# Graph layer and mixture of experts on one core: norm arithmetic on DVE, rows summed in memory, scatters on 128 partitions, three dense gelu buffers

## The chip, the cores and the metric

The kernel runs on one core of a Trainium2 chip. The metric is the device time of one execution in microseconds (us), the median of several runs. The engines are PE (TensorE), DVE (VectorE), ACT (ScalarE), POOL (GpSimd) and SP (SyncE, which here only issues transfers).

## What is computed

From the reference, cut to what matters. The adjacency matrix is dense in storage, 10000 x 10000 in float32, some 400 MB, and it is read once.

```python
x = x + relu(adj @ (item_feat @ W_item.T + b_item) + (layernorm(x) @ W_user.T + b_user))   # x: 10000 x 128
z = layernorm(x)
probs = softmax(z @ gate_w + gate_b)              # 8 experts
cw = the two largest probs of each row, elsewhere 0
for e in range(8):
    y = gelu(z @ W1[e] + b1[e]) @ W2[e] + b2[e]   # 128 -> 256 -> 128
    x = x + cw[:, e:e+1] * y
```

## The kernel before

**Blocks and chunks.** The 10000 rows are cut into 20 blocks of 500 (UB). For a block, the product with the adjacency runs over 26 chunks (CH), each of three slabs of 128 items; there are 520 chunks in all (NCH), numbered n, with b = n // 26 the block and c = n % 26 the position in it. For each chunk SP loads 750 KB into one of six buffers (`load_raw`, L296), ACT rounds it to a high part (`hi_chunk`, L738, the activation at L742, three buffers), DVE subtracts to get the low part (`lo_chunk`, L948, L952, two buffers), and PE does nine matmuls into one PSUM bank (`agg_chunk`, L487: three slabs times high x high at L496 and high x low at L497, then three times low x high at L501). ACT may start a chunk when PE is done with the chunk three before, DVE when PE is done with the one two before. SP may load chunk n once DVE is done with chunk n - 6.

**Everything else is threaded between the chunks.** All engines run the same loop over n, and constants give the position c of each other step: L54 to L57, and from L66 on the lists for the expert tiles. Steps of the block just finished (`post`, L681 on PE, L885 on ACT, L1198 on DVE) go beside the chunks of the next one. In their order: x1 is made on DVE at 1, turned and multiplied with the gate on PE at 1, its statistics taken on DVE at 4 (`stats2`, L980, L987) and those of the next block's input at 5 (`stats1`, L966, L971). POOL works out variance, power and shift of both in one call (`rstd`, L1289): eleven operations on 125 x 8 numbers, L1304 to L1320, of which L1316 is the power of -1/2. At 11 DVE takes the gate's logits (`logits`, L995, first operation L998), POOL raises e to them (`power`, L1322, L1324), ACT normalizes the rows at 12 (`ln2_norm`, L776, L787) and the next block's input at 15 (`ln1_norm`, L754), DVE does the softmax at 16 (L1011), the first and the second expert at 17 and 18 (`top`, L1029), and the slot numbers at 21 (`slots`, L1065). The rows of the blocks 0 to 16 (S = 17) are then scattered by expert into memory by POOL, eight indirect DMAs of 125 rows a block (`scatter`, L1339, L1346).

**Expert tiles.** Blocks 0 to 11 are one group, blocks 12 to 16 another. When a group's rows are scattered, a table of tiles is made on DVE (`table`, L1086), SP fills the gaps behind each expert's rows (`fill_end`, L374; it waits for all scatters of the group; at `FILL_AT`, L66), and tiles of 512 rows of one expert are worked off: 31 beside blocks 13 to 18, 17 beside blocks 18 and 19, the chunk of each in `W1_AT`. A tile is loaded by SP (`load_zt`, L342, weights and bias by `load_w`, L327, four bias buffers), turned on PE (`tile_turn`, L575), and goes through the first layer (`first_layer`, L583), gelu on ACT, second layer, and a turn back; DVE scales it (`y_out`, L1156, L1161, which waits for the sends of the tile two before), and POOL sends its rows to the array `rr` in memory by four indirect DMAs of 128 rows (`send`, L1351, L1355).

**The end.** Blocks 17 to 19 are done densely: 24 steps (ND), one for each block and expert (`dense_gelu`, L848; `scale`, L1168, L1172; `dense_round`, L860; `dense_rest`, L1174, L1176; on PE `first_layer` with L589 to L591, `dense_wbc`, L634, with L643, and `dense_w2`, L646, with L662 to L664). The gelu's output `dg` has two buffers. Beside them the two results of each row of the blocks 0 to 16 are summed: SP loads 256 KB of x1 (`comb_load`, L356), POOL adds two ranks of `rr` by an adding DMA each (`comb_add`, L1326, L1336), and SP stores the sum (`comb_store`, L365), 17 times; the dense blocks are stored by `out_store` (L370).

**What sets the order.** Every engine works through its own list in the order written, and waits are on semaphores, so a wait holds everything behind it on that engine.

Of the kernel before, what the change touches and what calls it, by code (L numbers as in the profile page):

```python
# [101 lines left out]
def build(nc, adj, adj_tail, x_tok, x_t, feat_t, feat_tail, wi_t, bb, bsel_d, wu_t, gate_w, gate_b,  # L102
          w12, b12, b2, ident_d, tri_d, w8_d, base_d, dest_d, sel_d, ints_d, out_s, out_d, zs, rr):
    ctx = ExitStack()
    with ctx:
# [27 lines left out]
        bias = sb("bias", [P, 4, 3])  # L133
# [35 lines left out]
        consts = sb("consts", [P, 4, 2 * SUBS])  # L169
# [5 lines left out]
        tsl = sb("tsl", [P, 2, SUBS, E])  # L175
        idx = sb("idx", [P, 2 * SUBS], I32)
# [36 lines left out]
        bn1_made, bn2_made, rs_step, rs_made = sem("bn1_made"), sem("bn2_made"), sem("rs_step"), sem("rs_made")  # L213
        ln1_normed, ln1_turned, ln1_copied, ln2_normed = (
# [31 lines left out]
        def dg(d):  # L246
            return g[:, 0:2 * UB] if d % 2 else flat[:, 0:2 * UB]
# [47 lines left out]
        def _(sp):  # L295
# [59 lines left out]

            def comb_load(p):  # L356
                if p == 0:
                    sp.wait_ge(lo_made, NCH)
# [5 lines left out]

            def comb_store(p):  # L365
                sp.wait_ge(comb_added[p % CB], 32 * (p // CB + 1))
                sp.dma_start(out_s[p * T:(p + 1) * T, :].rearrange("(p s) d -> p (s d)", s=SUBS), comb(p))\
                    .then_inc(comb_stored[p % CB], 16)
# [77 lines left out]
            for j in range(ND + 5):  # L446
                for p in range(S):
                    if COMB_OUT[p] == j:
                        comb_store(p)
# [495 lines left out]
        def _(dve):  # L945
# [275 lines left out]
            for n in range(LAST):  # L1221
# [47 lines left out]
                if d == 1:  # L1269
                    stats2(BLOCKS - 1)  # L1270
# [212 lines left out]
```

## Time and profile before

| | |
|---|---|
| median of 3 runs | 1539.0 us (1538.3 to 1539.04) |
| the profiled execution | 1538.6 us, of which the span of its instructions 1536.8 us |
| PE busy | 1469.6 us, 96% of the span |
| DVE, ACT, POOL busy | 1248.4, 1095.3, 885.7 us |
| transfers | 498.06 MB, 324 GB/s over the span |

The profile tells one execution. Times in it are microseconds from the first instruction. A line such as L952 is a line of the kernel; the releaser in brackets is what ended the idle time before an instruction. A matmul's record includes its way through the array, so matmuls overlap in the records, and the pace is the distance of their starts. Several buffers of one name are shown under one name.

### The profile page before, as it was taken

What the parts mean: (1) busy time and instruction counts of PE and PEld (TensorE: products, weight loads), DVE (VectorE), ACT (ScalarE), POOL (GpSimd) and SP (SyncE); (2) the same over time, 40 slices, a digit from 0 to 9 for tenths busy, and PEclk for the clock granted to TensorE, in tenths of its full rate; (3) what the DMA queues carried; (4) which work ended last, traced back from release to release, by engine and by line L of the source; (5) the groups of instructions that cost most, each with busy time, mean ns of one, the idle gap of its engine ahead of it and who ended that gap; (6) DMA issues with size and microseconds to landing.
All of it is one profiled execution on the core that took longest, in us unless ns stands there. A gap on an engine that the chain in (4) does not pass through costs nothing.

```text
span 1536.8 us, 20551 instructions
## 1 busy us (share of the span) xinstructions
PE 1469.6 (96%) x6682; PEld 1172.5 (76%) x6682; DVE 1248.4 (81%) x1627; ACT 1095.3 (71%) x1162; POOL 885.7 (58%) x630
## 2 busy tenths in 40 slices
PE   8999999999999999999998798999999999999997
PEld 6777787877877877778776587888888887877664
DVE  4778788888887887888888687889898988888775
ACT  4567677677677676776774677788887878788664
POOL 0105735637557457456364148777887887587662
PEclk9999999999999999999999899999999999999999
DMA  8879999999999999999997987889898899888399
GB/s 327 303 302 348 366 360 361 377 345 344 378 347 354 364 345 364 363 344 384 338 350 262 371 315 271 332 327 337 327 335 326 327 338 331 287 274 283 110 219 229
DMA packets 141720, 498.06 MB, mean 324 GB/s; under 512 B 33024, under 2 KB 39120, under 8 KB 141614
## 3 DMA queue, kind: packets, MB, share of 16 engines
q1 hardware_dynamic: 119694, 466.12, 82.3%
q0 software_dynamic: 21920, 30.64, 7.6%
q8 instruction: 53, 0.87, 0.2%
q14 instruction: 53, 0.43, 0.1%
HBM read 460.22 MB, written 36.31 MB: 323 GB/s over the span
## 4 chain that ended last, share of the span: by engine, by line
PE 49%; DVE 15%; POOL 14%; issue 8%; ACT 7%; DMA 5%; SPq 2%; POOLq 0%; ACTq 0%; DVEq 0%
PE p_agg L501 13%; PE p_agg L496 11%; PE p_agg L497 11%; DVE s_a_lo L952 9%; ACT s_a_hi L742 4%; POOL s_rs L1316 3%; DMA s_raw<-rr 3%; POOL s_rs L1304 2%; POOL zs L1346 2%; POOL s_rs L1312 1%; POOL s_rs L1305 1%; PE p_hid L478 1%; PE p_hid L589 1%; PE p_hid L591 1%; PE p_hid L590 1%
## 5 line engine op out<-in xcount | busy, mean ns | idle before, releaser
L952 DVE TENSOR_TENSOR s_a_lo<-s_raw,s_a_hi 128x1500 fp32r<-128x1500 f32 x520 | 885.8, 1718 | 139.4 <-PE p_agg L501 84.4
L742 ACT ACTIVATE s_a_hi<-s_raw 128x1500 fp32r<-128x1500 f32 x520 | 750.1, 1454 | 207.9 <-PE p_agg L501 184.9
L496 PE MATMUL p_agg<-s_a_hi,s_h_hi 128*128 128x500 f32 x1560 | 630.6, 404 | 10.2 <-ACT s_a_hi L742 10.1
L497 PE MATMUL p_agg<-s_a_hi,s_h_lo 128*128 128x500 f32 x1560 | 611.7, 392 | 0.0
L501 PE MATMUL p_agg<-s_a_lo,s_h_hi 128*128 128x500 f32 x1560 | 449.3, 396 | 33.9 <-DVE s_a_lo L952 31.0
L1346 POOL DMA_INDIRECT zs<-s_rows,s_idx x136 | 231.9, 1705 | 306.3 <-DVE s_idx L1080 211.8
L501 PEld LDWEIGHTS p_agg<-s_a_lo,s_h_hi 128*128 128x128 f32 x1560 | 290.2, 190 | 120.2 <-DVE s_a_lo L952 63.3
L496 PEld LDWEIGHTS p_agg<-s_a_hi,s_h_hi 128*128 128x128 f32 x1560 | 297.4, 191 | 75.3 <-ACT s_a_hi L742 17.9
L497 PEld LDWEIGHTS p_agg<-s_a_hi,s_h_lo 128*128 128x128 f32 x1560 | 297.3, 191 | 57.9 <-issue 3.2
L1355 POOL DMA_INDIRECT rr<-s_ysb,s_dests x192 | 277.4, 1445 | 102.7 <-issue 53.1
L1324 POOL TENSOR_TENSOR s_gt<-s_ebase,s_gt 125x32 f32<-125x32 f32 x20 | 130.8, 6538 | 37.2 <-DVE s_gt L1006 37.1
L1304 POOL TENSOR_TENSOR s_rs<-s_bn 125x8 f32<-125x8 f32 (+1 forms) x21 | 42.2, 2010 | 113.6 <-DVE s_bn L971 104.3
L1154 DVE TENSOR_TENSOR s_gl<-s_g,s_gh 128x1024 fp32r<-128x1024 f32 x48 | 58.8, 1226 | 51.3 <-ACT s_gh L832 51.3
L825 ACT ACTIVATE s_g<-p_hid,s_bias 128x512 f32<-128x512 f32 x96 | 60.6, 684 | 48.5 <-PE p_hid L591 48.5
L832 ACT ACTIVATE s_gh<-s_g 128x1024 fp32r<-128x1024 f32 x48 | 50.9, 1060 | 9.3 <-PE p_y L607 8.1
L1316 POOL TENSOR_TENSOR s_rs<-s_rs,s_consts 125x8 f32<-125x8 f32 (+1 forms) x21 | 55.7, 2655 | 1.6
L838 ACT ACTIVATE s_yt<-p_y,s_bias 128x512 f32<-128x512 f32 x48 | 32.6, 680 | 31.4 <-PE p_y L607 31.4
L787 ACT ACTIVATE s_rows<-p_agg,s_rs 125x128 f32<-125x128 f32 x80 | 30.0, 456 | 34.1 <-POOL s_rs L1320 34.1
L1336 POOL DMA_DIRECT2D s_raw<-rr x34 | 31.0, 1134 | 32.8 <-DMA s_raw<-out_s 16.7
L746 ACT ACTIVATE s_h_hi<-p_hid 128x384 fp32r<-128x384 f32 x26 | 12.8, 491 | 41.2 <-PE p_hid L478 41.2
L589 PE MATMUL p_hid<-s_zh,s_wt 128*128 128x512 f32 (+1 forms) x102 | 41.7, 409 | 0.4 <-ACT s_g L857 0.4
L818 ACT ACTIVATE s_zh<-p_tp 128x512 fp32r<-128x512 f32 x48 | 28.2, 587 | 19.0 <-PE p_hid L591 17.2
(214 smaller groups left out, 1478.6 us busy)
## 6 DMA issues: line engine op xcount, KB each, us to landing
s_raw<-adj SPq DMA_DIRECT2D x520, 750.0 KB, 6.6
s_wraw<-w SPq DMA_DIRECT2D x56, 256.0 KB
s_zt<-zs SPq DMA_DIRECT2D x48, 264.0 KB, 3.1
s_raw<-rr POOLq DMA_DIRECT2D x34, 256.0 KB, 6.7
s_xtok<-x_tok SPq DMA_DIRECT2D x20, 256.0 KB, 5.6
s_xt<-x_t SPq DMA_DIRECT2D x20, 250.0 KB, 6.7
zs<-s_early SPq DMA_DIRECT2D x18, 264.0 KB, 5.7
out_s<-s_x1s SPq DMA_DIRECT2D x17, 256.0 KB, 6.5
```

What stands on the lines that cost most here:

```text
L496: mm(o, h_hi[:, k * D:(k + 1) * D], hi, start=(k == 0), stop=False)
L497: mm(o, h_lo[:, k * D:(k + 1) * D], hi, start=False, stop=False)
L501: last = mm(o, h_hi[:, k * D:(k + 1) * D], a_lo[:, n % LOS, j * UB:(j + 1) * UB], start=False, stop=False)
L742: fn(a_hi[:, n % HIS, :], raw[:, n % RAW, :], ACT.Copy).then_inc(hi_made, 1)
L825: fn(g[:, h * T:(h + 1) * T], hid[h][:, :], ACT.Gelu, bias=bias[:, k % 4, h:h + 1])\
L952: tt(a_lo[:, n % LOS, :], raw[:, n % RAW, :], a_hi[:, n % HIS, :].bitcast(F32), ALU.subtract)\
L1154: tt(gl[:, :], g[:, :], gh[:, :].bitcast(F32), ALU.subtract).then_inc(gl_made, 1)
L1304: tt(row[0], even, odd, ALU.add)
L1316: tt(row[1], row[5], mhalf, ALU.pow).then_inc(rs_step, 1)
L1324: gp.tensor_tensor(gt[0:TS, 2, :], ebase[0:TS, :], gt[0:TS, 1, :], ALU.pow).then_inc(ez_made, 1)
L1346: gp.indirect_dma_start(out=zs[:, :], out_offset=bass.IndirectOffsetOnAxis(ap=idx[0:TS, j:j + 1].bitcast(U32), axis=0), in_=rows[k][0:TS, ...
L1355: gp.indirect_dma_start(out=rr[:, :], out_offset=bass.IndirectOffsetOnAxis(ap=dests[:, k % XR, s:s + 1].bitcast(U32), axis=0), in_=yrows(k ...
```

## The change

It does four things. The arithmetic of the norms, except the power, moves from POOL to DVE (`variances` and `shifts`, seven operations where POOL did ten), and the steps of a block behind it move forward: statistics of the input at 3, variances at 4, shifts at 7, logits at 8, rows normalized at 9, input normalized at 11, softmax 12, experts 13 and 14, slots 17. The sums of the rows are no longer made through SBUF at the end: POOL adds `rr` onto the output in memory, group 0 in six pieces of two blocks for each rank beside the tiles of group 1, the rest at the end in one piece for each rank. Scatters take 128 partitions, the last three rows going to spare rows past the end. The dense gelu gets a third buffer. With these go six bias buffers instead of four, and new places for fills, tiles and their loads; the first tile is at chunk 347 instead of 352, the first of group 1 at 477 instead of 482.

```diff
-X1_AT, X1T_AT, BN2_AT, BN1_AT, X1S_AT, LG_AT, LN2_AT = 1, 1, 4, 5, 4, 11, 12
-TAILHI_AT, TAILLO_AT, SOFT_AT, TOP1_AT, TOP2_AT, LN1_AT = 9, 10, 16, 17, 18, 15
-PREFIX_AT, LN1T_AT, SLOT_AT, LN1C_AT = 19, 17, 21, 20
-TABLE_AT = (21, 22, 23)
+X1_AT, X1T_AT, X1S_AT, BN1_AT, BN2_AT, FIN_AT, LG_AT, LN2_AT = 1, 1, 4, 3, 4, 7, 8, 9
+TAILHI_AT, TAILLO_AT, SOFT_AT, TOP1_AT, TOP2_AT, LN1_AT = 6, 7, 12, 13, 14, 11
+PREFIX_AT, LN1T_AT, SLOT_AT, LN1C_AT = 15, 13, 17, 16
+TABLE_AT = (17, 18, 19)
...
-FILL_AT = [(hi + 1) * CH + 6 for lo, hi in GROUPS]
-FIRST_W1 = [at + E // 2 + 4 for at in FILL_AT]
+FILL_AT = [(hi + 1) * CH + 4 for lo, hi in GROUPS]
+FIRST_W1 = [at + E // 2 + 1 for at in FILL_AT]
...
-W_LOAD = [0, 0] + [w + (6 if o + 2 < NTG[0] else 4) for o, w in enumerate(W1_AT[:NT - 2])] + [NCH - 3, NCH - 2]
-ZT_LOAD = [0, 0] + [max(W1_AT[k - 2] + 3, FILL_AT[k >= NTG[0]] + E // 2) for k in range(2, NT)]
-COMB_AT = [p if p < GROUPS[1][0] else p + 3 for p in range(S)]
-COMB_OUT = [6 + p if p < GROUPS[1][0] else p + 10 for p in range(S)]
+W_LOAD = [0, 0] + [w + 5 for w in W1_AT[:NT - 2]] + [NCH - 3, NCH - 2]
+ZT_LOAD = [0, 0] + [max(W1_AT[k - 2] + 5, FILL_AT[k >= NTG[0]] + E // 2) for k in range(2, NT)]
...
-            return g[:, 0:2 * UB] if d % 2 else flat[:, 0:2 * UB]
+            return (flat[:, 0:2 * UB], g[:, 0:2 * UB], flat[:, 2 * UB:4 * UB])[d % 3]
...
-                if d >= 2:
-                    act.wait_ge(gl_made, o - 1)
+                if d >= 3:
+                    act.wait_ge(gl_made, o - 2)
...
+            def variances(j):
...
+                tt(row[3], even, odd, ALU.subtract)
+                tt(row[4], bn[0:TS, lo:hi, 2], bn[0:TS, lo:hi, 5], ALU.add)
+                tt(row[0], even, odd, ALU.add).then_inc(rs_step, 1)
+                dve.wait_ge(rs_step, 2 * j + 1)
+                nc.vector.tensor_scalar(row[4], row[4], 1.0 / D, EPS, ALU.mult, ALU.add)
+                nc.vector.scalar_tensor_tensor(out=row[3], in0=row[3], scalar=0.25, in1=row[3],
+                                               op0=ALU.mult, op1=ALU.mult).then_inc(rs_step, 1)
+                dve.wait_ge(rs_step, 2 * j + 2)
+                tt(row[5], row[3], row[4], ALU.add).then_inc(var_made, 1)
+
+            def shifts(j):
...
+                dve.wait_ge(pow_made, j + 1)
...
+                nc.vector.scalar_tensor_tensor(out=rs[0:TS, 2, lo:hi], in0=rs[0:TS, 1, lo:hi], scalar=-0.5,
+                                               in1=rs[0:TS, 0, lo:hi], op0=ALU.mult, op1=ALU.mult)\
+                    .then_inc(rs_made, 1)
...
+            def add_rank(i, k):
+
+                blocks = GROUPS[0][1] // PAIRS
+                first, last = (i * blocks, (i + 1) * blocks) if i < PAIRS else GROUPS[1]
+                if k == 0:
+                    pool.wait_ge(rr_zeroed, 16 * 3)
+                    pool.wait_ge(x1_stored, 16 * last)
+                    for j in range(2):
+                        pool.wait_ge(sent[j], 16 * SUBS * tiles_of(j, NTG[0] if i < PAIRS else NT))
+                else:
+                    pool.wait_ge(rank0_added, 16 * (PAIRS + (i == PAIRS)))
...
+                gp.dma_start(out, new, max_dma_last_dim=8192, accum_op=ALU.add).then_inc((rank0_added, rank1_added)[k], 16)
...
-                            out_offset=bass.IndirectOffsetOnAxis(ap=idx[0:TS, j:j + 1].bitcast(U32), axis=0),
-                            in_=rows[k][0:TS, s, :], in_offset=None).then_inc(scattered, 16)
+                            out_offset=bass.IndirectOffsetOnAxis(ap=idx[:, j:j + 1].bitcast(U32), axis=0),
+                            in_=rows[k][:, s, :], in_offset=None).then_inc(scattered, 16)
...
                     if YOUT_AT[k] == n:
                         send(k)
-                        if k == NT - 3:
-                            rstd(BLOCKS)
...
+                        i = k - NTG[0] - 1
+                        if 0 <= i < 2 * PAIRS:
+                            add_rank(i % PAIRS, i // PAIRS)
+            power_of_rs(BLOCKS)
+            power(BLOCKS - 1)
+            add_rank(PAIRS, 0)
+            add_rank(PAIRS, 1)
```

## Rows read from the trace of the kernel before

**Rows 1.** Stretch: us, PE, PEld, DVE, ACT, POOL busy (instructions), clock, DMA share, GB/s.
```profile
98.70:762.10 663.40, 641.54 (x2872) 518.83 (x2871) 557.95 (x671) 468.51 (x418) 360.69 (x215) 0.99 0.96 358
...
824.50:910.40 85.90, 74.84 (x324) 59.03 (x323) 60.80 (x83) 55.98 (x59) 28.24 (x23) 0.94 0.84 309
...
1328.70:1434.00 105.30, 102.97 (x504) 82.72 (x502) 87.77 (x126) 84.19 (x108) 80.92 (x63) 1.00 0.76 256
```

**Rows 2.** Timeline of DVE in block 4: start us, us, line, tiles, idle before.
```profile
279.43 1.72 DVE L952 TENSOR_TENSOR s_a_lo<-s_raw,s_a_hi 128x1500 fp32r<-128x1500 f32 x1 [0.32 <-PE p_agg L501]
...
291.58 0.89 DVE L987 BATCH_NORM_STATS2 s_bn<-p_agg 125x6 f32<-125x128 f32 x4
...
308.55 0.19 DVE L998 TENSOR_TENSOR s_gt<-p_small,s_rs 125x32 f32<-125x32 f32 x1 [2.20 <-POOL s_rs L1320]
...
321.99 0.19 DVE L1034 TENSOR_TENSOR s_gt<-s_gt,s_w 125x32 f32<-125x32 f32 x1
...
339.50 1.72 DVE L952 TENSOR_TENSOR s_a_lo<-s_raw,s_a_hi 128x1500 fp32r<-128x1500 f32 x1 [0.30 <-PE p_agg L501]
```

**Rows 3.** Timeline of PE in block 4.
```profile
297.13 0.83 PE L501 MATMUL p_agg<-s_a_lo,s_h_hi 128*128 128x500 f32 x3
...
299.15 0.85 PE L501 MATMUL p_agg<-s_a_lo,s_h_hi 128*128 128x500 f32 x3
...
311.10 0.95 PE L501 MATMUL p_agg<-s_a_lo,s_h_hi 128*128 128x500 f32 x3 [1.59 <-DVE s_a_lo L952]
```

**Rows 4.** Timeline of POOL in block 4.
```profile
294.95 3.23 POOL L1304 TENSOR_TENSOR s_rs<-s_bn 125x8 f32<-125x8 f32 x1 [2.23 <-DVE s_bn L971]
...
304.74 3.14 POOL L1316 TENSOR_TENSOR s_rs<-s_rs,s_consts 125x8 f32<-125x8 f32 x1
...
309.49 6.84 POOL L1324 TENSOR_TENSOR s_gt<-s_ebase,s_gt 125x32 f32<-125x32 f32 x1 [1.04 <-DVE s_gt L1006]
```

**Rows 5.** Timeline of SP and of ACT in block 13.
```profile
838.73 1.49 SPq L379 DMA_DIRECT2D zs<-s_early  x2
...
858.05 9.20 SPq L299 DMA_DIRECT2D s_raw<-adj  x7
...
846.85 1.45 ACT L742 ACTIVATE s_a_hi<-s_raw 128x1500 fp32r<-128x1500 f32 x1 [8.74 <-DMA s_raw<-adj]
```

**Rows 6.** Timeline of DVE in block 14.
```profile
927.93 0.69 DVE L1161 TENSOR_TENSOR s_ysb<-p_y,s_probs 128x512 f32<-128x512 f32 x1 [5.80 <-DMA rr<-s_ysb,s_dests]
```

**Rows 7.** Timeline of the dense end, ACT and PE.
```profile
1517.57 1.25 ACT L857 ACTIVATE s_raw<-p_hid,s_dbias 128x500 f32<-128x500 f32 x2 [1.51 <-DVE s_h_hi L1176]
...
1521.25 1.25 ACT L857 ACTIVATE s_g<-p_hid,s_dbias 128x500 f32<-128x500 f32 x2 [1.50 <-DVE s_h_hi L1176]
...
1516.42 0.49 PE L643 MATMUL p_y<-s_cw,s_selr 16*128 16x500 f32 x1
...
1518.39 0.47 PE L589 MATMUL p_hid<-s_a_hi,s_h_lo 128*128 128x500 f32 x1
```

**Rows 8.** Timeline of the last us, DVE and SP.
```profile
1527.91 0.68 DVE L1181 TENSOR_TENSOR s_xt<-p_y,s_xt 128x500 f32<-128x500 f32 x1 [1.88 <-PE p_y L664]
...
1533.97 0.43 SPq L372 DMA_DIRECT2D out_d<-s_xt  x1
```

**Rows 9.** POOL: timeline of a block's scatters, and the page's group of sends.
```profile
814.36 1.29 POOL L1346 DMA_INDIRECT zs<-s_rows,s_idx  x1 [15.28 <-DVE s_idx L1080]
...
823.99 3.32 POOL L1346 DMA_INDIRECT zs<-s_rows,s_idx  x1 [5.71 <-issue]
...
834.37 1.19 POOL L1346 DMA_INDIRECT zs<-s_rows,s_idx  x1 [0.31 <-issue]
...
L1355 POOL DMA_INDIRECT rr<-s_ysb,s_dests x192 | 277.4, 1445 | 102.7 <-issue 53.1
```

**Rows 10.** The software queue on the page (packets, MB, share), and six us of block 4.
```profile
q0 software_dynamic: 21920, 30.64, 7.6%
...
297.40:303.40 6.00, 6.00 (x28) 5.02 (x27) 5.37 (x4) 4.68 (x5) 5.84 (x7) 1.00 1.02 412
```

More of the change, by code:

```diff
@@ L132, in build @@
         wt = sb("wt", [P, 3, 2, 2 * HID], F32R)
[L133 removed]
+        bias = sb("bias", [P, BIAS, 3])
         dbias = sb("dbias", [P, E, 3])
@@ L445, in _ @@
             load_w(NT + 3)
[L446 to L449, printed above, removed]
-                for p in range(S):
-                    if COMB_AT[p] == j:
-                        comb_load(p)
+            for j in range(ND + 4):
                 if j + 4 < E:
@@ L457, in _ @@
             sp.wait_ge(stored, 16 * (BLOCKS - S))
-            for i in range(CB):
-                sp.wait_ge(comb_stored[i], 16 * ((S - 1 - i) // CB + 1))
+            sp.wait_ge(rank0_added, 16 * (PAIRS + 1))
+            sp.wait_ge(rank1_added, 16 * (PAIRS + 1))
         @block.tensor
@@ L824, in gelu @@
                 for h in range(2):
-                    fn(g[:, h * T:(h + 1) * T], hid[h][:, :], ACT.Gelu, bias=bias[:, k % 4, h:h + 1])\
+                    fn(g[:, h * T:(h + 1) * T], hid[h][:, :], ACT.Gelu, bias=bias[:, k % BIAS, h:h + 1])\
                         .then_inc((gelu_half, gelu_done)[h], 1)
@@ L837, in y_evac @@
                     act.wait_ge(y_turned, k)
-                fn(yt[:, :], y[0][:, :], ACT.Identity, bias=bias[:, k % 4, 2:3]).then_inc(yt_made, 1)
+                fn(yt[:, :], y[0][:, :], ACT.Identity, bias=bias[:, k % BIAS, 2:3]).then_inc(yt_made, 1)
             def dz_round(q):
@@ L1243, in _ @@
                             .then_inc(b2_split, 1)
+                if n < NCH and c == BN1_AT + (4 if b == 0 else 0):
+                    stats1(b)
                 if b >= 1 and n < NCH:
@@ L1324, in power @@
                 gp.tensor_tensor(gt[0:TS, 2, :], ebase[0:TS, :], gt[0:TS, 1, :], ALU.pow).then_inc(ez_made, 1)
[L1326 to L1327 removed]
+            def add_rank(i, k):
+                blocks = GROUPS[0][1] // PAIRS
+                first, last = (i * blocks, (i + 1) * blocks) if i < PAIRS else GROUPS[1]
+                if k == 0:
                     pool.wait_ge(rr_zeroed, 16 * 3)
[L1329 to L1337 removed]
+                    pool.wait_ge(x1_stored, 16 * last)
[3 more added lines that the diff above has]
+                    pool.wait_ge(rank0_added, 16 * (PAIRS + (i == PAIRS)))
+                rows_of = slice(first * T, last * T), slice(k * RANK + first * T, k * RANK + last * T)
+                out, new = (t[rows, :].rearrange("(p s) d -> p (s d)", p=P) for t, rows in zip((out_s, rr), rows_of))
+                gp.dma_start(out, new, max_dma_last_dim=8192, accum_op=ALU.add).then_inc((rank0_added, rank1_added)[k], 16)
             def scatter(p):
@@ L1394, in _ @@
                         send(k)
-                        if k == NT - 3:
-                            rstd(BLOCKS)
-            for first, last in ((0, GROUPS[1][0]), (GROUPS[1][0], S)):
-                for p in range(first, last + 2):
-                    if p < last:
-                        comb_add(p, 0)
-                    if p - 2 >= first:
-                        comb_add(p - 2, 1)
-                    if p == 4:
-                        power(BLOCKS - 1)
+                        i = k - NTG[0] - 1
[5 more added lines that the diff above has]
+            add_rank(PAIRS, 1)
 def kernel(**inputs):
```

123 lines of the change are left out of this document (50 added, 73 removed).

## The prediction

> **What bounds the kernel now.** I read the busy time by stretch first. In blocks 1 to 11 PE is busy 641.5 of 663.4 us at a granted clock of 0.99, in block 19 103.0 of 105.3 us, but in block 13 only 74.8 of 85.9 us at 0.94 [rows 1]. So PE's own work sets the time, and a change can gain only what PE still waits for. Four such places matter here.
>
> *Blocks 1 to 12.* DVE's low-part subtractions mark the chunks. Block 4 runs from 279.43 to 339.50 us: 60.1 us for 26 chunks [rows 2]. A chunk that waits for nothing takes PE 2.02 us (the L501 groups at 297.13 and 299.15), 26 of them 52.9 us [rows 3]; the transposes, gate products, prefix sums and tail of a block come to about 3.1 us in the same timeline. So some 4.1 us of each block are waits and restarts. The largest is one of 1.59 us at 311.10, on DVE [rows 3]. DVE had itself idled 2.20 us before the gate's first operation, until POOL's L1320 [rows 2]. POOL's normalization takes eleven tiny operations, from 294.95 until just before the gate's 308.55: 13.5 us, of which L1304 takes 3.23 and the power of L1316 3.14 [rows 4]. About 3.5 of the 4.1 us come through DVE (this wait, and three bursts of gate operations later).
>
> *Blocks 13 and 14.* SP stops for the scatters before it fills the gaps in memory, and only at 838.73 issues the first fill; ACT waits 8.74 us for a chunk at 846.85; the seven chunk loads held behind SP's fills, weights and tile loads go from 858.05 on [rows 5]. In block 14 DVE waits 5.80 us to overwrite a row buffer that POOL, busy with a scatter, sends late [rows 6].
>
> *The dense end.* Its step is 3.68 us: ACT's gelu waits 1.51 us for DVE to finish with one of the two gelu buffers [rows 7].
>
> *The last us.* DVE's last result is ready at 1528.6, but its store is issued at 1533.97, behind the stores of the summed rows; the span ends at 1536.8 [rows 8].
>
> **Part by part.** *Norm arithmetic.* POOL keeps one power of some 3.1 us; DVE gets seven operations. One such operation takes 0.19 us [rows 2], some 0.22 with the gap behind it; three of the seven need nothing and overlap: about 0.9 us a block. They stand at chunks 4 and 7, the gate now starts at chunk 8, its softmax follows at 12, the tops at 13 and 14. POOL's power of the exponentials takes 6.84 us [rows 4], inside the four chunks (8.1 us) left for it; before, five. Does DVE keep up? Back to back it needs 1.64 us a chunk where PE needs 2.03, so it gains 0.4 a chunk, and since it works two buffers ahead it may be 1.7 us late before PE notices (one chunk and six matmuls, 3.4, less its own 1.7). Lateness after each chunk: 3 (statistics, 0.8, [rows 2]) 0.4; 4 (statistics and the new arithmetic, 1.6) 1.6; 6, 0.8; 7 (tail 0.7, shift 0.1) 1.2; 8 (gate 0.8) 1.6; 11, 0.4, raised to 1.1 by ACT, which now normalizes at 9 and 11 (2.1 and 1.6 us); 12 (softmax 0.9) 1.6; 13 (top, 1.2) 2.1 with PE's transposes taken off; 14 (1.0) 2.3. Over the limit of 1.7 that is 1.0 us of waiting, 1.4 with restarts. So 3.5 becomes 1.4: 2.1 us x 12 blocks = **25 us**. Ends: 0.5 a block if the denser bursts give most of it back (6), all of 3.5 (42).
>
> *Scatters on 128 rows, eight positions 17 instead of 21.* Before, the eight of a block take 21 us, from 814.36 to 835.6, with one pause of 5.71 us for no engine [rows 9]; the sends, with 128 rows, take 1.45 us each and idle 53.1 us in 192 for no engine, 0.3 each [rows 9]. Bounds for a block's eight: 14 us like the sends, 21 as now; I take 14, since the sends are the same operation in shape. The three added rows an operation go to spare rows and are 2.4% more packets. [...]
>
> *Start of the tiles.* The scatter now starts four chunks (8 us) earlier and ends 6 earlier still, while SP asks two chunks (4 us) sooner: its 11 us wait goes away, or shrinks to about 6. What stays is SP's own issue time: some 19 us from the first fill to the load at 858.05, for five chunks that PE would do in 10 [rows 5]. Of about 16 us lost here I take back **8** (3 with scatters as now, 12 at best). The send behind the scatter is now ahead of it (positions 354 and 355): the 5.80 us wait goes, with PE's slow restart **5** (0 to 6).
>
> *Rows summed in memory.* Removed: 34 adding DMAs, 17 loads and 17 stores of 256 KB. Added: beside group 1's tiles twelve adding DMAs of 512 KB in memory, and two of 1.3 MB at the end. POOL pays about 1 us to issue one; it has 9.4 us for a tile against 7.0 for four sends, so that is covered, as is the wait of the second rank for the first. The DMA engines are the open cost. Plain transfers reach 412 GB/s at a full share: 2.4 us a MB. The software queue moved 30.64 MB in 7.6% of the span, 117 us, 3.8 a MB; were all above 2.4 due to the 8.9 MB of additions, these would cost 7.2 [rows 10]. I take 5.5, midway between those two: 35 us for 6.3 MB in about 105 us of blocks 18 and 19. These need 256 GB/s, 0.62 of the DMA time at the best rate (0.76 as recorded, [rows 1]). 0.62 and 0.33 make 0.95: nearly full, with six chunk buffers as a cushion. I charge **4 us** (0 to 24: 0.76 and 0.47 make 1.23).
>
> *Three gelu buffers.* The loop gelu, scale, rest of 3.6 us opens to two steps. Next is PE: 1.97 us from L643 at 1516.42 to L589 at 1518.39 [rows 7] and six matmuls at the 0.225 of a chunk's nine, 1.35: 3.32; I take 3.35. DVE has 2.23 and ACT 2.1 us a step, about 3 with the weights. The first four steps stay DVE's (row outputs, statistics, weights, now 0.9 more). 19 steps x 0.33 = 6.3, less 2.2 of transposes and bias products that the old waits covered, and 1.3 at the last item: **5.5** (2 to 14 if the step falls to 3.0). The last norm's power now waits on POOL for the last sends, to about 1450; DVE needs it at about 1453: covered by 3 us.
>
> *The end.* The last store follows DVE by 0.1 us instead of 5.4: **5** (3 to 6). The two late additions (2.6 MB, 14 to 19 us from about 1467) end 25 us ahead.
>
> *At nothing:* the index DMA and copy in block 0, six bias buffers instead of four (they take waits from SP), tiles moved five chunks forward (the same PE work); the tile load is placed two chunks later, which leaves it 10 us for 3, and if that cover goes PE stands for the difference per tile.
>
> **Sum.** 25 + 8 + 5 - 4 + 5.5 + 5 = 44.5 us off the profiled run's 1538.6 (span 1536.8), 0.4 below the median 1539.0: 1494; some 1 us more where DVE's small waits in blocks 15 to 18 go. **1493 us**, 3.0% faster.
>
> **Rivals.**
> *A, the norm's wait only moves.* Three bursts, now nearer to each other, and DVE at about 93% of PE's pace, speak for it; the walk above against. 0.5 a block: 1493 + 19 = 1512.
> *B, full queues in blocks 1 to 12.* The DMA share there is 0.96 at 358 GB/s [rows 1], and 58 us a block needs 371; were the queues full, the block could not shorten: 1493 + 25 = 1518. But six us at 412 GB/s stand in the same blocks [rows 10]. [...]
> *C, the DMA queues fill in blocks 18 and 19.* At 7.2 to 8 us a MB 10 to 25 us lost: 1503 to 1518.
> *D, slower than before.* [...] At x us a MB the loss is 6.3x less the idle 40 us; 1539 is passed from x = 14, twice the upper bound. At 16 it is 61 us: 1550.
> *E, more is gained.* Scatters, fills and dense steps all at their good ends, DVE never late: 1475.
> *F, the change doesn't do what it says:* POOL, still held by DMA issue, delivers the power after chunk 7, DVE's shift waits as the gate did, and the start of the tiles stays: 1520.
>
> **Chances.** Forecast 0.55 (its own range 1482 to 1504), A 0.11, B 0.04, C 0.09, D 0.04, E 0.10, F 0.04, no change at all 0.03. A measurement of this kernel can tell about 0.2%, 3 us. Faster 0.93, within 0.2% 0.03, slower 0.04. The range takes in the forecast, A, B and C, and E down to 1475: **1475 to 1518**.
>
> **What would show it.** Blocks 1 to 12 at about 58.0 us, with no DVE wait on POOL before the gate; DVE bursts at chunks 13 and 14 as PE's only waits; scatters without the 6 us pause; ACT's waits for chunk loads in block 13 below 6 us in all; dense steps of 3.35 us; the last store within 0.5 us of DVE's last result; block 19 with a DMA share near 0.95 and no ACT wait for chunks. A block still at 60, or chunk waits of ACT in blocks 18 and 19, would make it wrong.

## The result and the profile after

The changed kernel takes 1501.1 us (median of four runs, 1501.0 to 1506.6) against 1538.7 for the kernel before on the same chip (1536.0 to 1539.0): a ratio of 0.977, 95% interval 0.974 to 0.979. Forecast were 1493 us and a range of 1475 to 1518. The profiled run took 1501.0 us with a span of 1499.2; the sum of the prediction had said 1494.

I cut both traces where DVE subtracts the first low part of a block. "Tiles" is the stretch from there in block 13 to the start of the last subtraction of all; "end" is the rest of the span.

| us, profiled runs | before | after | gained | forecast |
|---|---|---|---|---|
| block 0 | 87.5 | 84.3 | 3.2 | 0 |
| blocks 1 to 12 | 725.8 | 696.6 | 29.2 | 25 |
| tiles, blocks 13 to 19 | 604.7 | 610.8 | -6.1 | 8 + 5 - 4 + 1 |
| end | 107.5 | 96.1 | 11.4 | 5.5 + 5 |

The time came out within 0.6% of the forecast partly by luck: the tiles missed by 16.1 us and had the wrong sign, and 8.3 us of that were made up by block 0 (3.2), by blocks 1 to 12 (4.2) and by the end (0.9). The busy time by stretch for the changed kernel: blocks 1 to 11, then 13, 14, 18 and 19 (stretch: us, PE, PEld, DVE, ACT, POOL busy, clock, DMA share, GB/s).

```profile
95.70:732.90 637.20, 632.36 (x2873) 514.04 (x2872) 566.42 (x749) 466.91 (x419) 262.82 (x109) 1.00 0.98 370
792.30:877.60 85.30, 76.25 (x345) 61.10 (x344) 64.81 (x95) 59.39 (x65) 29.48 (x19) 0.96 0.92 334
877.60:956.30 78.70, 78.64 (x381) 65.05 (x380) 69.60 (x105) 64.14 (x75) 56.26 (x34) 1.00 0.95 329
1202.90:1303.40 100.50, 91.81 (x432) 74.08 (x430) 78.98 (x119) 73.01 (x90) 61.00 (x40) 0.98 0.89 311
1303.40:1403.10 99.70, 92.48 (x446) 73.83 (x445) 79.97 (x123) 75.79 (x97) 72.04 (x54) 1.00 0.92 290
```

Eleven blocks take 637.2 us where they took 663.4 [rows 1], each 57.9. But block 13 is as long as before; with the tiles five chunks earlier it also holds 345 matmuls where it held 324 [rows 1]. In blocks 18 and 19 PE stands idle for 8.7 and 7.2 us, with the granted clock at 0.98 and 1.00. Over all the tiles PE has the same 2765 matmuls before and after (busy 584.2 and 582.0 us), and its idle time rises from 20.6 to 28.8 us.

The norm's steps in block 4, on POOL and on DVE, are to be read beside [rows 2, 4]:

```profile
283.49 3.08 POOL L1313 TENSOR_TENSOR s_rs<-s_rs,s_mhalf 125x8 f32<-125x8 f32 x1 [13.52 <-DVE s_rs L982]
291.69 6.84 POOL L1318 TENSOR_TENSOR s_gt<-s_ebase,s_gt 125x32 f32<-125x32 f32 x1 [5.12 <-DVE s_gt L1011]
```

```profile
282.59 0.17 DVE L974 TENSOR_TENSOR s_rs<-s_bn 125x8 f32<-125x8 f32 x1
...
283.24 0.17 DVE L982 TENSOR_TENSOR s_rs<-s_rs 125x8 f32<-125x8 f32 x1
...
290.76 0.18 DVE L1003 TENSOR_TENSOR s_gt<-p_small,s_rs 125x32 f32<-125x32 f32 x1
```

POOL's 13.5 us have become 3.1, DVE's six operations last 0.8 us, and the gate's first operation follows with no wait on POOL. PE's waits for DVE in blocks 1 to 11 (us in total, times, longest), before and after:

```profile
PE p_agg L501 <- DVE s_a_lo L952: 20.4, 19, 1.9
```

```profile
PE p_agg L476 <- DVE s_a_lo L927: 3.6, 11, 0.3
```

The wait of 1.6 us that every block had at its chunk 12 is gone; what is left is 0.3 us at chunk 15.

PE's waits at the start of the two groups of tiles are new. The column in brackets is PE's idle time and what ended it; below it is the load that the last of them waits for.

```profile
820.04 1.12 PE L555 MATMUL p_tp<-s_ident,s_zt 128*128 128x128 f32 x4 [4.99 <-DMA s_zt<-zs]
...
1227.45 0.66 PE L555 MATMUL p_tp<-s_ident,s_zt 128*128 128x128 f32 x4 [1.45 <-DMA s_zt<-zs]
...
1244.18 0.66 PE L555 MATMUL p_tp<-s_ident,s_zt 128*128 128x128 f32 x4 [4.26 <-DMA s_zt<-zs]
```

```profile
1234.85 0.34 SPq L346 DMA_DIRECT2D s_zt<-zs  x1
```

The rows of that tile arrive 9.3 us after their load is issued. And the end, ACT's gelus, DVE's last result and SP's last store [rows 7, 8]:

```profile
1479.17 1.25 ACT L832 ACTIVATE s_raw<-p_hid,s_dbias 128x500 f32<-128x500 f32 x2 [1.45 <-PE p_hid L566]
1482.48 1.24 ACT L832 ACTIVATE s_raw<-p_hid,s_dbias 128x500 f32<-128x500 f32 x2 [1.14 <-PE p_hid L566]
```

```profile
1495.83 0.68 DVE L1186 TENSOR_TENSOR s_xt<-p_y,s_xt 128x500 f32<-128x500 f32 x1 [1.87 <-PE p_y L639]
```

```profile
1496.54 0.33 SPq L352 DMA_DIRECT2D out_d<-s_xt  x1
```

The step is 3.31 us instead of 3.68, ACT now waits for PE and no longer for DVE, and the span ends 2.7 us behind DVE's last result instead of 8.2.

### The profile page after: what moved, and what is told of

It reads as the page before. It is cut to its first block, busy times and chain, and to the rows that moved or that the text cites. A ratio compares the mean times of both kernels' runs of the same rounds, so it can differ in the third digit from the quotient of the medians.

```text
span 1499.2 us, 20455 instructions
## 1 busy us (share of the span) xinstructions
PE 1451.7 (97%) x6682; PEld 1165.8 (78%) x6682; DVE 1263.0 (84%) x1775; ACT 1093.4 (73%) x1162; POOL 709.5 (47%) x397
## 4 chain that ended last, share of the span: by engine, by line
PE 67%; DVE 12%; ACT 8%; issue 7%; DMA 3%; SPq 2%; POOL 1%; ACTq 0%; DVEq 0%; POOLq 0%
PE p_agg L476 17%; PE p_agg L471 15%; PE p_agg L472 15%; DVE s_a_lo L927 8%; ACT s_a_hi L717 4%; PE p_hid L564 2%; PE p_hid L566 2%; PE p_hid L565 2%; ACT s_xtok L733 2%; ACT s_rows L762 1%; PE p_hid L453 1%; PE p_y L580 1%; PE p_y L582 1%; PE p_y L581 1%; PE p_agg L487 1%
## 5 line engine op out<-in xcount | busy, mean ns | idle before, releaser
L476 PEld LDWEIGHTS p_agg<-s_a_lo,s_h_hi 128*128 128x128 f32 x1560 | 287.1, 188 | 97.4 <-DVE s_a_lo L927 40.2
L1351 POOL DMA_INDIRECT rr<-s_ysb,s_dests x192 | 274.1, 1427 | 165.1 <-DVE s_ysb L1166 111.6
L1313 POOL TENSOR_TENSOR s_rs<-s_rs,s_mhalf 125x8 f32<-125x8 f32 (+1 forms) x21 | 56.2, 2678 | 232.6 <-DVE s_rs L982 232.5
L800 ACT ACTIVATE s_g<-p_hid,s_bias 128x512 f32<-128x512 f32 x96 | 60.7, 686 | 44.2 <-PE p_hid L566 38.7
L813 ACT ACTIVATE s_yt<-p_y,s_bias 128x512 f32<-128x512 f32 x48 | 32.9, 685 | 31.4 <-PE p_y L582 23.4
L555 PE MATMUL p_tp<-s_ident,s_zt 128*128 128x128 f32 x192 | 29.6, 278 | 15.8 <-DMA s_zt<-zs 10.7
L564 PE MATMUL p_hid<-s_zh,s_wt 128*128 128x512 f32 (+1 forms) x102 | 41.6, 408 | 0.4 <-issue 0.4
L566 PE MATMUL p_hid<-s_zl,s_wt 128*128 128x512 f32 (+1 forms) x102 | 40.2, 394 | 0.0
L565 PE MATMUL p_hid<-s_zh,s_wt 128*128 128x512 f32 (+1 forms) x102 | 40.1, 393 | 0.0
```

The source lines that it names most:

```text
L476: last = mm(o, h_hi[:, k * D:(k + 1) * D], a_lo[:, n % LOS, j * UB:(j + 1) * UB], start=False, stop=False)
L564: mm(hid[h][:, 0:n], w_hi, hi, start=True, stop=False)
L565: mm(hid[h][:, 0:n], w_lo, hi, start=False, stop=False)
L566: last = mm(hid[h][:, 0:n], w_hi, lo, start=False, stop=True)
L800: fn(g[:, h * T:(h + 1) * T], hid[h][:, :], ACT.Gelu, bias=bias[:, k % BIAS, h:h + 1])\
L1351: gp.indirect_dma_start(out=rr[:, :], out_offset=bass.IndirectOffsetOnAxis(ap=dests[:, k % XR, s:s + 1].bitcast(U32), axis=0), in_=yrows(k ...
```

## The experiments

Twelve kernels ran, each with three rounds beside the kernel before. Ratios are to the kernel before on the same chip (1535.8 to 1537.9 us there); stretches are those of the table, from the profiled run. Kernels 1 and 2 are built on the kernel before, the others on the changed one.

**1. The norm part alone.** The kernel before, with `variances`, `shifts` and the power as in the change and the four lines of positions from X1_AT to TABLE_AT (VAR_AT is BN2_AT); nothing else.

```diff
-                    if c == BN1_AT:
-                        rstd(b)
+                    if c == VAR_AT:
+                        power_of_rs(b)
```

> The kernel before with the norm arithmetic on DVE and the steps of a block at their new positions; fills, tiles, loads, scatters on 125 rows, sums through SBUF and two gelu buffers as before. Theory (the norm part gives the whole gain of blocks 0 to 12): blocks 1 to 12 take 696 to 700 us as in the changed kernel (before 725.8), block 0 84.3 (before 87.5); the scatters come 8 us earlier too, so SP's first fill in block 13 and the send in block 14 no longer wait, some 8 to 13 us. In all 1538.6 - 29 - 3 - 10 = 1497, 1490 to 1505. Rival (part of the gain of blocks 1 to 12 comes from the other parts, fewer scatter packets and the pause): blocks 1 to 12 stay above 705 us, in all 1507 to 1515.

1498.0 us, ratio 0.974 (0.970 to 0.977). Block 0 86.0, blocks 1 to 12 696.6, tiles 597.3, end 106.4, span 1498.1. So the norm part by itself is as fast as the whole change: 38.7 us of span, 29.2 in blocks 1 to 12 and 7.4 among the tiles.

```profile
97.90:735.00 637.10, 632.22 (x2873) 513.96 (x2872) 566.53 (x749) 466.97 (x419) 261.44 (x109) 1.00 0.99 370
794.40:876.30 81.90, 72.89 (x326) 57.43 (x325) 61.63 (x90) 56.31 (x59) 28.10 (x16) 0.98 0.91 334
1291.70:1391.70 100.00, 97.16 (x479) 79.22 (x478) 85.50 (x130) 83.15 (x106) 74.61 (x49) 1.00 0.78 262
```

The theory held (1497 expected). Its blocks 1 to 11 equal the changed kernel's within 0.1 us, so neither the scatters' width nor their packets play a part there. The other three parts of the change then give 10.3 us in the end and lose 13.5 among the tiles. Most of the remaining experiments look for these 13.5.

**2. The arithmetic without the moves.** As 1, every step at its old place.

```diff
+VAR_AT, FIN_AT = 5, 9
```

> The kernel before with the norm arithmetic on DVE alone; every step stays at its old position (variances at 5, shifts at 9, gate at 11). Theory (the wait of DVE for POOL before the gate is what the block lost; the moved steps only start the scatters earlier): blocks 1 to 12 as short as with the moved steps, 58.0 to 58.4 us each, the start of the tiles as before, 1538.6 - 28 = 1510. Rival (the steps' new spacing carries part of it): blocks at 58.8 to 59.5 us, in all 1518 to 1526.

1502.3 us, 0.979 (0.974 to 0.983). That is faster than both expectations (1510, and 1518 to 1526). Blocks 1 to 12 take 693.3 us, less than with the moved steps, and the first eleven of them 57.6 each.

```profile
96.00:729.70 633.70, 629.45 (x2872) 516.23 (x2871) 563.88 (x748) 467.76 (x418) 250.05 (x105) 1.00 1.00 374
```

The gain of the blocks is the arithmetic's; the moves cost 3.3 us there. What they bring is at the tiles, 606.0 against 597.3: the scatters end earlier, and SP waits for them 7.8 us in kernel 1 and 12.9 here. The DMA share of 1.00 at 374 GB/s, in a shorter block than the change has, also disposes of rival B.

**3. No additions beside the tiles.** The rows of blocks 0 to 11 stay unsummed in the output.

```diff
-                        if 0 <= i < 2 * PAIRS:
+                        if False:
```

> The changed kernel without the twelve additions of group 0 beside group 1's tiles; the rows of blocks 0 to 11 in out_s are left unsummed, the two additions at the end stay. Theory (the additions cost what was charged, about 4 us, by load on the DMA engines): the stretch of blocks 18 and 19 up to the last subtraction, 200.2 us, falls to 196, in all 1497. Rival 1 (they are the reason of the stage's extra 14 us of PE waits): the stretch falls to 186 to 190, in all 1488 to 1491. Rival 2 (they cost nothing; the waits come from the tiles' places): the stretch stays within 1.5 us of 200.2, in all 1500 to 1501.

1504.2 us, 0.979 (0.975 to 0.982). Blocks 18 and 19 take 102.7 and 99.6 us (with the additions 100.5 and 99.7):

```profile
1203.20:1305.90 102.70, 92.77 (x432) 74.91 (x431) 79.12 (x120) 73.08 (x90) 60.26 (x38) 0.97 0.85 298
1305.90:1405.50 99.60, 92.39 (x446) 73.77 (x445) 79.83 (x122) 75.70 (x97) 64.09 (x44) 1.00 0.70 234
```

Leaving the additions out gains nothing; the two blocks even take 202.3 us instead of 200.2, and the whole 3 us more. That is outside every range expected (rival 2 had 1.5 us around 200.2), and rival 2, that the additions cost nothing, is the one that it fits; where the 2 us come from is not shown. The additions do load the DMA engines: the shares 0.89 and 0.92 fall to 0.85 and 0.70, by the trace 24.9 us of full load for 6.3 MB, 4.0 us a MB. There was room for that. ACT's waits for chunks in block 18 are 4.0 us without the additions and 2.7 with them, and in block 19 there are none in either.

**4. The first tiles three chunks later.**

```diff
-FIRST_W1 = [at + E // 2 + 1 for at in FILL_AT]
+FIRST_W1 = [at + E // 2 + 4 for at in FILL_AT]
```

> The changed kernel with the first tile of each group three chunks later behind the fills (8 chunks as before the change, now 5), the tile loads still 5 chunks behind the tile two before. Theory (PE turned the first tiles before SP had loaded them): the PE waits for the rows of a tile at 814.7 (4.99 us) and at 1225.6 and 1239.5 (1.45 and 4.26 us) go, in all -8 us, 1493. The tiles of group 1 then stand 2.24 instead of 2.41 chunks apart, which may give back 2: 1493 to 1496. Rival (the waits come from the tile load placed two chunks later, not from the first tile): one of the three goes at most, 1499 to 1503.

1496.4 us, 0.973 (0.970 to 0.976). As the theory said, the three waits at the groups' starts are gone. The tiles fall from 610.8 to 604.9 us; block 18 from 100.5 to 92.5, while block 19 rises to 102.3 and has 2.4 us of waits for rows (3.4 in both blocks, not the 3.9 of the next expectation). The edit also makes the distances of group 1's tiles more even (three of 3 chunks instead of six), so it does not price the first tiles' place alone. The end was 100.8 us in the profiled run, which was the slowest of four (1494.9 to 1500.5).

**5. As 4, and the tile loads two chunks earlier.**

```diff
-ZT_LOAD = [0, 0] + [max(W1_AT[k - 2] + 5, ...
+ZT_LOAD = [0, 0] + [max(W1_AT[k - 2] + 3, ...
```

> The changed kernel with the first tiles 3 chunks later and the tile loads 3 instead of 5 chunks behind the tile two before; only the fills stay 2 chunks earlier than before the change (and with them the first tile, 350 instead of 352). From block 13 to the last subtraction the changed kernel takes 610.7 us, with the first tiles 3 later 604.9, with all places as before 592.4. Theory (the late tile loads are most of what is left, in blocks 18 and 19, where PE still waits 3.9 us for rows): 597 to 601. Rival 1 (the early fills are it: SP asks for the scatters two chunks early and holds the chunk loads behind them, so block 13 stays at 81.8 instead of 77.4): 600 to 604.9. Rival 2 (both together only): 592 to 596.

1495.6 us, 0.973 (0.971 to 0.975). PE waits for no rows any more, yet the tiles take 604.2 us: the waits for rows gave way to waits for DVE (next experiment). The number lies in the range of rival 1, but its cause, the early fills, is only a part at most: block 13 takes 80.1 us where the old places give 77.4, and the next experiment finds more elsewhere.

**6. As 5, and group 1's tiles at an even distance.**

```diff
-... (NCH - 2 - FIRST_W1[1]) / NTG[1]]
+... 36 / NTG[1]]
```

> The kernel with the first tiles 3 later and the tile loads 3 behind (stretch from block 13 to the last subtraction 604.2 us, of it blocks 18 and 19 92.5 and 103.4), with group 1's tiles 36/17 = 2.12 chunks apart instead of 2.24: one distance of 3 chunks among them instead of three (the changed kernel has six, all places as before one). Theory (PE's waits for DVE's low part of the rows and for DVE's scaled tile, 3.5 and 3.2 us in block 19, come where the distances change between 2 and 3 chunks): block 19 falls to 100 to 101 us though it holds no fewer tiles, the two waits to 3 us together, in all 1492. Rival (what is left of the 12 us to the old places comes from the fills two chunks earlier and group 0's tiles alone): block 19 stays at 103 or more, in all 1495 to 1496.

1492.5 us, 0.973 (0.970 to 0.976), the profiled run 1489.0. Against 5 the intervals overlap, so the time alone shows no gain and the reading rests on the trace. Block 19 falls from 103.4 to 98.5 us, below the 100 to 101 expected. PE's waits there (us in total, times, longest), first for 5, then for 6:

```profile
PE p_tp L555 <- DVE s_zl L1144: 3.5, 2, 2.6
PE p_y L590 <- DVE s_ysb L1166: 3.2, 1, 3.2
```

```profile
PE p_y L590 <- DVE s_ysb L1166: 1.2, 2, 0.8
PE p_tp L555 <- DVE s_zl L1144: 0.8, 1, 0.8
```

I read it so: where the distance between tiles is 3 chunks once and 2 the next time, steps of two tiles meet in one chunk and PE waits for DVE. The changed kernel has six such distances of 3 among group 1's sixteen, the kernel before had one.

**7. All places of fills, tiles and loads as before the change.** Norm, additions, scatters and gelu buffers stay changed.

```diff
-FILL_AT = [(hi + 1) * CH + 4 for lo, hi in GROUPS]
+FILL_AT = [(hi + 1) * CH + 6 for lo, hi in GROUPS]
```

and with it the old lines for `FIRST_W1`, `W_LOAD` and `ZT_LOAD`.

> The changed kernel with the places of fills, first tiles, weight loads and tile loads as before the change (fills 2 chunks later, first tile 8 instead of 5 chunks behind them, tile loads 3 chunks behind the tile two before); norm, additions in memory, scatters, three gelu buffers and six bias buffers as changed. The norm alone, with the old places, had 597.3 us from block 13 to the last subtraction, the changed kernel 610.7. Theory (the places alone cost those 13 us): the stretch takes 596 to 600 us, the dense end stays at 96, in all 1501 - 13 = 1488, 1485 to 1491. Rival (the wider scatters, the additions or the sixth bias buffer have a share): the stretch stays at 604 or more, in all 1494 to 1501.

1490.9 us, 0.970 (0.969 to 0.972). The tiles take 592.4 us, 18.4 less than in the changed kernel and below the 596 to 600 expected; the whole gains only 10 us, in part because the end takes 100.3 us instead of 96.1 (see 12).

```profile
793.50:870.90 77.40, 71.42 (x322) 56.78 (x322) 61.52 (x89) 56.38 (x60) 25.61 (x15) 0.98 0.94 350
1194.10:1285.90 91.80, 89.80 (x429) 72.74 (x427) 79.51 (x121) 72.62 (x89) 51.66 (x34) 1.00 0.92 332
1285.90:1386.00 100.10, 97.24 (x479) 79.28 (x478) 85.45 (x131) 83.28 (x106) 80.40 (x60) 1.00 0.98 315
```

SP's first fill is issued at 798.70, with fills placed two chunks later than in the changed kernel, where it is at 798.87. So the scatters decide when filling begins, and asking earlier only means that SP waits 7.5 us for them instead of 2.1, with the chunk loads behind it (11.1 before the change).

**8. Two gelu buffers.**

```diff
-            return (flat[:, 0:2 * UB], g[:, 0:2 * UB], flat[:, 2 * UB:4 * UB])[d % 3]
+            return g[:, 0:2 * UB] if d % 2 else flat[:, 0:2 * UB]
```

> The changed kernel with two gelu buffers in the dense end, as before. Theory (the third buffer gave about 6 us, the earlier last store 5): the 48 gelus, 79.6 us from first to last in the changed kernel, take 85 to 87, and the kernel 1507. Rival 1 (PE's clock falls in the end for want of work, and the third buffer gave more through that): 88 us or more, in all 1510 or more. Rival 2 (the step of the dense end was set by the sums' transfers, now gone): the gelus take 81 us or less, in all 1502.

1514.4 us, 0.985 (0.983 to 0.986). The gelus take 86.7 us from first to last instead of 79.6, the end 103.0 instead of 96.1. The step is 3.68 again:

```profile
1491.78 1.25 ACT L832 ACTIVATE s_raw<-p_hid,s_dbias 128x500 f32<-128x500 f32 x2 [1.51 <-DVE s_h_hi L1181]
...
1495.46 1.25 ACT L832 ACTIVATE s_g<-p_hid,s_dbias 128x500 f32<-128x500 f32 x2 [1.51 <-DVE s_h_hi L1181]
```

The gelus take what the theory said (85 to 87), but the whole is 7 us above its 1507. The third buffer is worth 6.9 us in the end; the rest of this run's distance, 6.6 us, lies elsewhere: block 0 took 87.7 us and the tiles 613.8, by the same instructions as in the changed kernel.

**9. The rows summed through SBUF at the end.** `comb_load`, `comb_add` and `comb_store` of the kernel before instead of `add_rank`, their buffers moved behind the third gelu buffer.

```diff
-            c0 = 2 * UB + p % CB * T
+            c0 = 4 * UB + p % CB * T
```

> The changed kernel with the rows summed as before: none beside the tiles, at the end 17 loads, 34 additions and 17 stores through SBUF (buffers moved to make room for the third gelu buffer). Theory (the additions beside group 1's tiles cost nothing, as leaving them out showed, and the sums at the end only hold up the last store): the stretch from block 13 to the last subtraction stays within 3 us of 610.7, the dense end grows from 96.1 by 5 us for the late last store, in all 1506. Rival (the transfers of the end also slow the dense steps): the gelus take 83 us or more instead of 79.6, in all 1510 or more. Second rival (the sums, 18.3 MB at a share of 1.0, now outlast the shorter dense end): the span ends 8 us or more behind DVE's last result.

1512.7 us, 0.985 (0.983 to 0.986). The gelus take 79.6 us, as in the changed kernel, but the end 104.3. SP's queue and DVE's last result:

```profile
1493.71 10.83 SPq L371 DMA_DIRECT2D out_s<-s_raw  x5
1504.58 0.43 SPq L376 DMA_DIRECT2D out_d<-s_xt  x1
```

```profile
1496.22 0.68 DVE L1216 TENSOR_TENSOR s_xt<-p_y,s_xt 128x500 f32<-128x500 f32 x1 [1.87 <-PE p_y L669]
```

The last store is issued 7.7 us behind the result, behind five stores of sums. With two gelu buffers that was 5.4 [rows 8]: in a shorter end the sums stand out further. The span ends 10.9 us behind the result, as the second rival said (8 or more), and the tiles take 611.0 us as the theory said. The new sums save 8.2 us in the end once there is a third buffer.

**10. Scatters on 125 partitions.**

```diff
-                            in_=rows[k][:, s, :], in_offset=None)
+                            in_=rows[k][0:TS, s, :], in_offset=None)
```

> The changed kernel with the scatters on 125 partitions as before (the spare indices stay unused). Theory (the width changes nothing but the number of packets, as the pause of 5.9 us is there with 128 rows as well): blocks 1 to 12 stay at 57.9 us each, POOL's idle time ahead of the scatters stays within 10 us of 49.4, in all 1501, 1499 to 1503. Rival (the wider scatter is what halved that idle time, 94.2 us before): it is back at 80 us or more, SP's first fill comes 4 to 7 us later than 798.87, the start of the tiles loses 2 to 5 us, in all 1504 to 1506.

1507.5 us, 0.980 (0.979 to 0.982). My theory fell: POOL's idle time before the scatters is back at 93 us, as the rival said, and the loss is larger than its 1504 to 1506. The tiles take 619.1 us instead of 610.8; SP's first fills come at 801.93 and 1213.48 (changed kernel 798.87 and 1205.85). I had misread the trace: POOL's idle time of 49.4 us before 123 scatters is 0.30 each and only two pauses of 5.9 and 6.6 us. With 125 rows there are ten, here and in the kernel before. The pauses of this kernel are before its 10th, 19th, 28th, 37th, 46th, 55th and 64th scatter, then the 82nd and 91st: every nine scatters (the 73rd begins a block, where POOL waits anyway; the tenth pause, of 2.5 us, comes when sends already lie between). Of the changed kernel they are before the 29th and the 85th, and scatter 93 takes 5.4 us. One of each kernel:

```profile
205.70 1.99 POOL L1342 DMA_INDIRECT zs<-s_rows,s_idx  x1 [6.09 <-issue]
```

```profile
325.66 2.27 POOL L1342 DMA_INDIRECT zs<-s_rows,s_idx  x1 [5.89 <-issue]
```

The software queue's packets over one block's eight scatters, for 125 rows and for 128:

```profile
q0 software_dynamic: 640, 0.54, 5.1%
```

```profile
q0 software_dynamic: 256, 0.54, 4.1%
```

With 125 rows the data of the eight are 120 packets of eight rows and 40 of one row: five groups of 25 rows a scatter. With 128 they are 128 packets of eight rows, 16 a scatter. The rest of the 640 are 264 packets of 32 bytes and 216 of 4 bytes, in all 80 packets a scatter; with 128 rows the rest are 128 packets of 4 bytes, in all 32 a scatter. The three added rows thus do not make 2.4% more packets, as the prediction had it, but 60% fewer. The trace does not tell the engines apart, so how the packets are spread over them is not shown.

The loss is in blocks 13 and 18 (89.2 and 104.9 us against 85.3 and 100.5), where SP fills the gaps. The granted clock was lower too: in block 13 of this kernel 0.90 against 0.96.

```profile
794.00:883.20 89.20, 78.36 (x345) 63.88 (x344) 65.05 (x95) 59.30 (x65) 31.21 (x20) 0.90 0.89 318
```

**11. Half of `dynamic_dma_scratch_size`.**

```diff
-    nc = bacc.Bacc("TRN2", ..., dynamic_dma_scratch_size=4096)
+    nc = bacc.Bacc("TRN2", ..., dynamic_dma_scratch_size=2048)
```

> The changed kernel with half the memory for the descriptors that POOL writes for its indirect transfers (2048 instead of 4096). [...]

1503.8 us, 0.977 (0.975 to 0.979), by the time not to be told from the changed kernel (0.974 to 0.979), so the reading rests on the trace. POOL's idle time before 123 scatters is 63.0 us instead of 49.4, and what changes is the distance of the pauses. There are five instead of two, of 5.1 to 5.8 us, before the 15th, 29th, 43rd, 71st and 85th scatter: every 14 scatters (the 57th begins a block, where POOL waits anyway), where with 4096 the two lie 56 apart (twice 28). One of them:

```profile
215.51 1.05 POOL L1342 DMA_INDIRECT zs<-s_rows,s_idx  x1 [5.05 <-issue]
```

Half the size, half the distance: the pauses depend on this argument of the program. How is not shown, and two things stay open. The scatters of this run landed 4.5 to 10.7 us after their issue, so of the 14 or 28 between two pauses, spread over two to four blocks of 58 us, most had landed long before the pause. And no pause is seen in any of these kernels once sends lie between the scatters, apart from the 2.5 us above.

**12. As 7, second and third gelu buffer exchanged.** In 7 ACT began the second dense gelu 7.7 us after the first, and the end took 100.3 us:

```profile
1392.62 1.25 ACT L832 ACTIVATE s_raw<-p_hid,s_dbias 128x500 f32<-128x500 f32 x2 [1.22 <-issue]
1400.36 1.25 ACT L832 ACTIVATE s_g<-p_hid,s_dbias 128x500 f32<-128x500 f32 x2 [5.97 <-remote]
```

```diff
-            return (flat[:, 0:2 * UB], g[:, 0:2 * UB], flat[:, 2 * UB:4 * UB])[d % 3]
+            return (flat[:, 0:2 * UB], flat[:, 2 * UB:4 * UB], g[:, 0:2 * UB])[d % 3]
```

> The kernel with all places as before (1488.1 us in its profiled run, median 1490.9) with the second and third gelu buffer of the dense end exchanged, so that the second dense gelu writes to a chunk buffer and the third to the buffer that the last expert tile used. There ACT began the second gelu 7.74 us after the first instead of 3.67. Theory (it waits for the buffer of the last tile): the step falls to 3.7 and in all 4 us are gained, 1487 median. Rival (the wait has nothing to do with the buffer, an instruction fetch or a semaphore that came late): a step of over 4.5 us stays among the first three, in all 1489 to 1492.

1484.4 us (1483.8 to 1486.4), 0.966 (0.964 to 0.968): the fastest of all, and clear of the changed kernel (0.977) and of kernel 7 (0.970). The second gelu follows 3.67 us after the first and the end takes 95.8. That the buffer was the cause is not shown. Of the kernels with the old order, 4 starts as slowly (steps of 4.79 and 5.68 us, and an end of 100.8), while the changed kernel and 5 have no such pause (3.67 and 2.58 us). It stays open.

## Why the prediction was right or wrong

**Norm arithmetic, 25 us: right, somewhat low.** The block came out at the 58 us forecast, with no wait of DVE for POOL before the gate (57.9). The 4 us more come from the base: I took block 4's 60.1 us [rows 2] for all twelve, and they average 60.5 (725.8 / 12). The walk over the chunks was too dark: PE waits for DVE 0.3 us in a block, at chunk 15, not 1.0 at chunks 13 and 14. And the recorded waits do not give the whole gain: they fall by 1.5 us a block (20.4 to 3.6 in eleven), the block by 2.4. The other 0.9 is in no recorded wait and was not taken apart. (26 chunks of 2.02 us are 52.5, not 52.9, so waits and restarts were 4.5 us of block 4 and not 4.1.) Experiment 2 shows that the arithmetic alone does it, and that the new spacing, for which the walk was made, costs 0.3 us a block.

**Block 0, 3.2 us: not a part of the change.** Kernels with the same block 0 as the changed one took between 83.9 and 87.7 us in it.

**Scatters: the term was right, the count of packets wrong.** In nine of the first eleven blocks the last of the eight started 14.9 us or less behind the first, close to the 14 taken; in the two with a pause, 21.0. The pause did not vanish ("scatters without the 6 us pause"): two of ten stayed. A block's scatters have 256 packets instead of 640. The 128 rows are worth 8.3 us of the tiles, in the changed kernel's places (experiment 10).

**Start of the tiles, 8 + 5 us: half of it failed.** The send in block 14 waits no longer, and that block falls by 6.8 us: right. Block 13 gave 0.6 instead of 8. SP's wait for the scatters shrank to 7.5 us, much as forecast ("or shrinks to about 6"); ACT still waits 11.5 us in all for chunks (19.7 before) where I wrote below 6. What took the gain was the line "at nothing": a wait of 5.0 us for the first rows, and 21 more matmuls in this block, some 4.7 us (an estimate, at 0.225 us each), which are missing in block 19 and so are no loss.

**"At nothing": the step that failed.** It put two things at nothing: that the tile load, two chunks later, has 10 us for 3, and that tiles moved forward are the same PE work. The load behind a burst of chunk loads took 9.3 us, and for the first tiles of each group there were no 10: the rows are turned three chunks before the first layer, at fill place + 2, and SP loads them at fill place + 4. PE stood for the difference, as the step said, 10.7 us in three waits. The new places also spread group 1's tiles unevenly. Old places give 18.4 us of the tiles back (experiment 7): 5.9 with the first tiles' place, three wide distances fewer among them (experiment 4), 0.7 with the tile loads (experiment 5) and 4.1 with the even distance (experiment 6 against 5). The rest, 7.7 us, lies in blocks 13 to 17, which take 410.5 us in the changed kernel, 408 to 410 in kernels 4 to 6 and 400.6 in kernel 7. A part of that is no loss but work that falls into other blocks: PE has 1890 matmuls and 397.7 us busy there in the changed kernel, 1860 and 390.5 in kernel 7. I have not taken the rest apart, since the fills, the weight loads and group 0's tiles moved together.

**Rows in memory, -4 us: 0.** The price of 5.5 us a MB was about right: the software queue's packets took 7.0% of 1499.2 us with the twelve additions and 4.8% of 1501.6 without, 32.9 us for 6.3 MB or 5.2 a MB, while all queues together had 4.0 a MB less to do. What was too high is the loss charged for it: block 19 had a share of 0.92 and no wait of ACT for chunks, and those of block 18 did not go when the additions went. Rivals C and D are out. (The 10 to 25 us of C do not agree with the formula of D, which gives 5 to 10 for 7.2 to 8 us a MB.)

**Three gelu buffers, 5.5 us: 6.9 measured** (experiment 8); the step is 3.31 to 3.35 as forecast. Which part of the term was too low is not measured; the one with no row behind it is the 2.2 us for covered transposes and bias products. **The last store, 5 us: 5.5** (the span ended 8.2 us behind DVE's last result, now 2.7), and 8.2 where the new sums are taken away alone. The two measured parts make 12.4 us and the end gained 11.4, so they do not simply add.

Rival A would have needed 0.5 us a block, B is refuted by 57.6 us a block, E by the tiles, F by the trace of block 4.

## What to carry to other kernels

A part that costs nothing in the old place can cost most of the gain in the new one: price every moved constant against the slowest transfer the trace shows behind a burst (here 9.3 us, where 3 were reckoned with), and check for each loop of places that what is used comes after what is loaded at its first index. Keep interleaved items at even distances (block 19 took 98.5 us with them and 103.4 without). Of several edits made together try each alone: here one gave all of the net gain, and the new places cost 18 us among the tiles.

## What the runs showed of the hardware

- **POOL's pauses between scatters.** A pause of 5 to 7 us comes every 9 scatters with 125 rows (kernel 10 and the kernel before), at multiples of 28 with 128 (the changed kernel and kernel 7), and every 14 with 128 and half of `dynamic_dma_scratch_size`. A limit on the packets of all scatters together does not give both widths: 28 scatters of 32 packets, 896, went without a pause, and 10 of 80, 800, did not. What is counted is not shown.
- **After a wait PE ran slower.** In kernel 7 PE waits 4.50 us at the start of the dense end, and then its matmuls start 0.42 us apart instead of 0.23 for some 6 us; the granted clock of the stretch is 0.78.

```profile
1394.00:1406.00 12.00, 7.50 (x28) 5.17 (x27) 6.49 (x15) 4.43 (x8) 6.72 (x7) 0.78 0.24 72
```

- **Additions in memory.** The changed kernel's 1088 packets of 8192 bytes took 47.2 us of all 16 engines for 8.9 MB, 5.3 us a MB. The additions into SBUF of the kernel before, 4352 packets of 2048 bytes, took 52.1 us for the same 8.9 MB, 5.8 a MB and not the 7.2 of the prediction's upper bound. So additions onto memory were no dearer than those into SBUF.
